# A fused GNN and mixture-of-experts kernel: six chunks of rows fetched one row at a time by the sync engine

## The reference

```python
def _L0_gnn_ref(node_repr, weight, bias, edge_index, edge_types):     # 53125 edges, 8 relations
    h_all = jnp.einsum('ni,roi->rno', node_repr, weight)
    src, dst = (edge_index[0], edge_index[1])
    msgs = h_all[edge_types, src]
    messages = jax.ops.segment_sum(msgs, dst, num_segments=node_repr.shape[0])
    return messages + bias
...
edge_index = jnp.stack([src, dst])
x = x + _L0_gnn_ref(_layernorm(x, axis=-1), L0_gnn_weight, L0_gnn_bias, edge_index, edge_type_8)
x = x + _L0_ffn_ref(_layernorm(x, axis=-1)[None], L0_ffn_gate_w, L0_ffn_gate_b, L0_ffn_w1, L0_ffn_w2, L0_ffn_w3)[0]
```

## Time and profile before

| | us |
|---|---|
| three runs | 925.81, 927.8, 933.22 |
| their median | 927.8 |
| the profiled execution's own time | 927.84 |
| its span in the profile | 926.1 |
| mean granted TensorE clock, as a share of full speed | 0.928 |

### The profile page before, as it was taken

One profiled execution on the slowest core, in us unless ns is written; L12 is line 12 of the kernel. 1 busy time (PEld: TensorE's weight loads), 2 busy tenths in 40 slices (PEclk: granted clock), 3 DMA queues, 4 the chain that ended last, 5 costly groups with the idle time before them and its releaser, 6 DMA issues.

```text
span 926.1 us, 17827 instructions
## 1 busy us (share of the span) xinstructions
PE 725.9 (78%) x4528; PEld 617.5 (67%) x4529; DVE 520.1 (56%) x1447; ACT 300.0 (32%) x466; POOL 659.9 (71%) x614
## 2 busy tenths in 40 slices
PE   0135778888887898877889887388999999999980
PEld 0123567666776677766777666267888888888870
DVE  6687746465454654546554577883444444344438
ACT  5423233252222433234332333222333333233323
POOL 7774777777777777777777760249788796987772
PEclk9997799899998999989999999589999999999995
DMA  9872444454444433343334334166756664763546
GB/s 207 245 224 63 146 145 145 144 178 145 144 144 137 133 104 103 106 130 107 102 106 131 106 95 147 34 203 236 222 186 227 205 197 167 229 210 95 158 135 188
DMA packets 91487, 141.91 MB, mean 153 GB/s; under 512 B 13197, under 2 KB 65889, under 8 KB 91456
## 3 DMA queue, kind: packets, MB, share of 16 engines
q0 software_dynamic: 25680, 70.16, 26.2%
q1 hardware_dynamic: 48854, 56.28, 18.9%
q10 hardware_dynamic: 16922, 15.15, 5.1%
HBM read 108.61 MB, written 32.93 MB: 153 GB/s over the span
## 4 chain that ended last, share of the span: by engine, by line
PE 39%; POOL 25%; issue 17%; DMA 11%; DVE 3%; ACT 2%; SPq 1%; DVEq 1%; POOLq 0%; ACTq 0%
POOL got L573 21%; PE ps L1677 15%; PE ps L1659 8%; PE ps L1525 8%; DMA got<-x_tab,gidx 5%; PE ps L1537 5%; DMA acc<-in_x 2%; PE ps L1685 2%; POOL x_sb L618 2%; DMA store<-in_L_gnn_weight 2%; PE ps L1643 1%; DVE ps L1450 1%; POOL part L607 1%; DMA y_tab<-ffn 1%; DMA x_tab<-x_sb 1%
## 5 line engine op out<-in xcount | busy, mean ns | idle before, releaser
L573 POOL DMA_INDIRECT got<-x_tab,gidx x388 | 370.9, 956 | 127.1 <-issue 113.1
L1525 PE MATMUL ps<-hot,got 125*128 125x256 f16 x1700 | 222.0, 292 | 88.3 <-DMA got<-x_tab,gidx 69.7
L1525 PEld LDWEIGHTS ps<-hot,got 125*128 125x128 f16 x1700 | 172.9, 104 | 133.2 <-issue 45.9
L1095 DVE TENSOR_TENSOR store<-store,ps 128x512 f32 x150 | 102.6, 684 | 187.8 <-PE ps L1525 153.2
L1677 PE MATMUL ps<-part,operands 128*128 x696 | 180.7, 409 | 5.3 <-POOL part L607 4.1
L1537 PE MATMUL ps<-part,store 128*128 128x256 f32 x800 | 183.7, 388 | 0.5 <-DVE acc L1106 0.5
L1537 PEld LDWEIGHTS ps<-part,store 128*128 128x128 f32 x800 | 154.0, 195 | 21.0 <-issue 0.5
L1677 PEld LDWEIGHTS ps<-part,operands 128*128 128x128 f32 x696 | 129.6, 193 | 33.4 <-issue 6.1
L1077 DVE TENSOR_SCALAR hot<-key_row,pass,drel 125x256 f16<-125x256 f16 x425 | 124.4, 358 | 11.2 <-issue 11.1
L1659 PE MATMUL ps<-part,operands 128*128 x696 | 97.8, 289 | 3.2 <-DVE operands L1389 3.2
L607 POOL TENSOR_TENSOR part<-store,part 128x2048 fp32r<-128x2048 f32 (+1 forms) x28 | 98.0, 3499 | 2.3
(11 more groups left out here) (250 smaller groups left out, 658.0 us busy)
## 6 DMA issues: line engine op xcount, KB each, us to landing
store<-in_L_ffn_w SPq DMA_DIRECT2D x48, 512.0 KB
y_tab<-ffn SPq DMA_DIRECT2D x9, 896.0 KB, 4.5
y_tab<-ffn ACTq DMA_DIRECT2D x58, 128.0 KB
xs_tab<-x_sb SPq DMA_DIRECT2D x14, 512.0 KB, 3.2
ffn<-xs_tab ACTq DMA_DIRECT2D x55, 128.0 KB
got<-x_tab,gidx POOLq DMA_INDIRECT x388, 2.7
acc<-in_x SPq DMA_DIRECT2D x5, 560.0 KB
x_tab<-got SPq DMA_DIRECT2D x5, 560.0 KB
```

Source lines behind the costliest of these rows:

```text
L573: nc.gpsimd.indirect_dma_start(got[:, c, :], None, x_tab, bass.IndirectOffsetOnAxis(ap=gidx[:, col:col + 1], axis=0)).then_inc(gathered[g] ...
L1095: v.tensor_tensor(window, window, ps[:, WIN_BANK[g], :].rearrange("p (q n) -> p q n", n=WIN), ALU.add).then_inc(win_added, 1)
L1525: last = mm(ps[:, WIN_BANK[g], k * KEYS:(k + 1) * KEYS], got[0:CE, c, a * DIM + k * P:a * DIM + (k + 1) * P], hot[0:CE, g % HOT, c - c0, : ...
```

## The change

Column 15 of the even turns 12, 14, 16, 18, 20 and 22 is no longer gathered by Pool. SyncE loads the 125 source numbers of such a chunk into registers, 25 at a time, and issues a DMA of one row (1 KB, one partition) for each. The rows go to `far_room`, two places of one chunk each that take turns, in memory that held the sort keys and the bias before. TensorE waits for all 125 rows (`far_in`) and takes the weights of that chunk from `far_room`. For that its loop over pairs is written twice: pairs 1 to 5 without, pairs 6 to 11 with the new operand, whose address comes from a register. SyncE may fill a place again once the last group of the turn that used it is done: chunks 2 to 5 wait for turns 12, 14, 16 and 18. The `y_tab` stores are let go two to a turn, and the first four batches of `store_x2` now stand behind the new loop.

```diff
@@ sync engine
-                sp.wait_ge(moved_on, n + 2)
+                sp.wait_ge(moved_on, n // 2 + 2)
...
+            sp.wait_ge(edges_done, 1)
+            far_chunks = early[FAR_FIRST:FAR_FIRST + 2 * FAR, HELD - 1, :].rearrange("(t a) e -> t a e", a=2)[:, 0, :]
+            sp.dma_start(far_src, far_chunks).then_inc(early_in, 16)
+            sp.wait_ge(early_in, 3 * 16)
             sp.wait_ge(counts_ready, 5)
...
+            for n in range(X_LOADS):
+                sp.wait_ge(batch_moved[n], 4 * 16)
+            rows_at = [sp.alloc_register(f"row_at{n}") for n in range(ROWS_AT)]
+
+            def far_rows(m, v0):
+                for p0 in range(0, CE, ROWS_AT):
+                    sp.reg_load(rows_at, far_src[m:m + 1, p0:p0 + ROWS_AT])
+                    for n, row in enumerate(rows_at):
+                        at = nc.s_assert_within(sp.snap(row, min_val=0, max_val=NODES - 1), 0, NODES - 1,
+                                                skip_runtime_bounds_check_because="sources are nodes")
+                        sp.dma_start(far_room[p0 + n:p0 + n + 1, m % 2, :], x_tab[bass.ds(at, 1), :]).then_inc(far_in, 16)
+
+            with sp.Fori(0, visits, TILES) as v0:
+                for m in range(FAR):
+                    freed = FAR_FIRST + 2 * (m - 2) + 1 if m >= 2 else 0
+                    sp.wait_ge(group_done, (v0 + freed) * NG + NG)
+                    sp.sem_inc(tiles_begun, 1)
+                    far_rows(m, v0)
+                    sp.wait_ge(far_in, (v0 // TILES * FAR + m + 1) * CE * 16)
+                    sp.sem_inc(tiles_begun, 1)
 
             for n in range(X_LOADS - 1):
                 store_x2(n)
@@ Pool
-                    for c in range(c0, min(c1, HELD - turn % 2)):
+                    for c in range(c0, min(c1, HELD - (turn % 2 or turn in range(FAR_FIRST, FAR_LAST + 1)))):
@@ TensorE, window
+                elif far:
+                    pe.wait_ge(far_in, (sweep * FAR + pair - FAR_FIRST // 2 + 1) * CE * 16)
+                    pe.wait_ge(held_ready, v0 + turn + 1)
+                    far_at = pe.snap(pair % 2, min_val=0, max_val=1)
...
+                            d0 = a * DIM + k * P
+                            rows = got[0:CE, c, d0:d0 + P]
+                            if far and c == HELD - 1:
+                                rows = far_room[0:CE, bass.ds(far_at, 1), d0:d0 + P].rearrange("p s d -> p (s d)")
@@ TensorE, the loop
-                    with nc.Fori(1, TILES // 2, engines=PE_ONLY, hint_back_edge=True, head_slot={pe.engine: 0}) as pair:
-                        for at in range(2):
-                            turn(pair * 2 + at, at, pair)
+                    for p0, p1, far in ((1, FAR_FIRST // 2, False), (FAR_FIRST // 2, TILES // 2, True)):
+                        with nc.Fori(p0, p1, engines=PE_ONLY, hint_back_edge=True, head_slot={pe.engine: 0}) as pair:
+                            for at in range(2):
+                                turn(pair * 2 + at, at, pair, far=far)
```

More of the change, by code:

```diff
@@ L61 @@
 EARLY = TILES + ODD
+FAR_FIRST, FAR = 12, 6
+ROWS_AT = 25
+FAR_LAST = FAR_FIRST + 2 * (FAR - 1)
 HOT = NG
@@ L184, in build @@
         key_c, bias = early_room[:, 0:CHUNKS], early_room[:, CHUNKS:CHUNKS + DIM]
+        far_room = early_room[:, 0:2 * DIM].bitcast(F16).rearrange("p (s d) -> p s d", s=2)
+        far_src = early_room[0:FAR, 2 * DIM:2 * DIM + CE].bitcast(I32)
         drel = sb("drel", [P, CHUNKS])
@@ L285, in build @@
         early_in = sem("early_in")
+        far_in = sem("far_in")
         early_rows = sem("early_rows")
@@ L1507, in _, with window @@
                 turn_weights(n)
-            def window(v0, turn, g, sweep=0, pair=0, odd=False):
+            def window(v0, turn, g, sweep=0, pair=0, odd=False, far=False, passed=0):
                 c0, c1 = GROUPS[g]
@@ L1518, in window @@
                     pe.wait_ge(held_ready, v0 + turn + 1)
+                elif far:
+                    pe.wait_ge(far_in, (sweep * FAR + pair - FAR_FIRST // 2 + 1) * CE * 16)
+                    pe.wait_ge(held_ready, v0 + turn + 1)
+                    far_at = pe.snap(pair % 2, min_val=0, max_val=1)
                 else:
-                    pe.wait_ge(gathered[g], (sweep * (TILES - ODD) + pair + 1) * 16)
+                    pe.wait_ge(gathered[g], (sweep * (TILES - ODD - FAR) + pair - passed + 1) * 16)
                     pe.wait_ge(held_ready, v0 + turn + 1)
@@ L1524, in window @@
                         for a in range(2):
-                            last = mm(ps[:, WIN_BANK[g], k * KEYS:(k + 1) * KEYS], got[0:CE, c, a * DIM + k * P:a * DIM + (k + 1) * P],
+                            d0 = a * DIM + k * P
+                            rows = got[0:CE, c, d0:d0 + P]
+                            if far and c == HELD - 1:
+                                rows = far_room[0:CE, bass.ds(far_at, 1), d0:d0 + P].rearrange("p s d -> p (s d)")
+                            last = mm(ps[:, WIN_BANK[g], k * KEYS:(k + 1) * KEYS], rows,
                                       hot[0:CE, g % HOT, c - c0, :], start=(c == c0 and a == 0), stop=(c == c1 - 1 and a == 1))
@@ L1582, in _, with turn @@
                         window(v0, 1, g)
-                    def turn(i, at, pair, norm=True):
+                    def turn(i, at, pair, norm=True, far=False):
                         window(v0, i, 3)
                         window(v0, i, 4)
-                        window(v0, i, 5, sweep, pair, odd=at == 1)
+                        window(v0, i, 5, sweep, pair, odd=at == 1, far=far and at == 0)
                         if norm:
@@ L1604, in _ @@
                     window(v0, t, 4)
-                    window(v0, t, 5, sweep, ODD)
+                    window(v0, t, 5, sweep, ODD, passed=FAR)
                     pe.wait_ge(choice_step, (b * GEN_W + w) * SWEEP_STEPS + 2 * CHOICE_STEPS)
```

## The result

The changed kernel takes 1057.1 us (median of 4 runs) against 927.5 (4 runs): a ratio of 1.1395, 95% interval 1.1357 to 1.1433. It is 130 us slower; the forecast was 1005 with an upper end of 1047. The direction was right and the time was 10 us outside the range. The profiled execution took 1056.1 us, its span is 1054.4.

A forecast was written before the change was run, and what follows sets the result against it. Pool bounded the edge stage; SyncE's row DMAs were to become the bound, moving the stage's end from 554.85 to 633 us. 927.84 + 78 = 1006, given as 1005; range 919 to 1047, the forecast's own 966 to 1047.

The forecast's parts named there:

- Pool sets the edge stage's pace, and six gathers less are worth up to 7.5 us.: Edge stage, second half: Pool waits for nobody, one gather per 1.25 us; removing six takes 7.5 us off the end.
- one queue of six that ends at the later of 191.5 + 6T and 321.1 + 4T: SyncE's six chunks, begun at 191.5 us, third not before turn 12 ends at 321.1; predicted end 601.3 us.
- T: SyncE's time for one chunk of 125 rows, loads and last landing included: 68.3 us, from 47.6 to 79.0.
- A row: 0.518 us.: SyncE's price per one-row DMA: issue 0.33, register calculation 0.054, MOVE 0.029, three gaps of 0.035; bounds 0.353 to 0.604.
- The lower bound of T: Cheapest chunk on SyncE: 125 x 0.353 + 3.5 = 47.6 us, with no register work at all.
- The loads: 5 x 0.307 = 1.5 us.: SyncE's five loads of 25 source numbers a chunk, priced like single-value loads; at 25 loads' price, 32 us more.
- a rival at 0.05: "Worse": a load costs as 25 loads, or SyncE waits for its instructions; T = 100, total 1195; chance 0.05.
- The upper end, 1047.: Top of the range for the total, at T = 75: stage ends at 673, +119.
- The stage's end, 32 us behind the late group.: Edge stage ends at 633, after turn 22's last group waits for SyncE's queue to end at 601.3: +78 us.
- The expert stage as before.: After the edge stage: the expert stage was expected to have its old length.
- y_tab's stores, `store_x2` and the doubled loop at nothing.: Two y_tab stores a turn, store_x2 behind SyncE's last chunk, TensorE's loop written twice: all covered by slack, taken as nothing.
- the rows just fit: SyncE issues a row in at most 0.344 us, T under 46.5, no chunk late, total 920; chance 0.19.

The follow-up runs named there:

- The run with aligned loads: Changed kernel with each set of 25 source numbers beginning at a multiple of 32 numbers instead of 25: 996.5 us against 931.5, ratio 1.0709.
- the other kernels with 382 gathers: Four variants of the changed kernel: loads realigned (996.5 us), one plain DMA a chunk (926.2), 105 DMAs a chunk (962.9), Pool's code padded with semaphore increments (1054.4).

## Why the prediction was right or wrong

- *Pool sets the edge stage's pace, and six gathers less are worth up to 7.5 us.* Right in kind: where the rows are in time the last gather starts 4.8 us earlier for six gathers fewer (or 7.0, less the 2.2 of the later start), 2.9 for two, 3.6 for four.
- *SyncE becomes the bound; one queue of six that ends at the later of 191.5 + 6T and 321.1 + 4T.* Right, in both regimes. With the measured T = 74.2 it gives 636.7; TensorE's last late group began at 638.7. At T = 55.5 the second term held to the tenth, with the release taken from that trace.
- *A row: 0.518 us.* Too dear. It measured 0.416. The instructions were the right ones (0.044 and 0.029 us), but a DMA of one row holds the sequencer 0.225 us, below the 0.300 that I took as the floor. I had excluded anything cheaper than the cheapest issue of the trace, all of which spread over 12 to 128 partitions, though I named the row as the smallest transfer there is. Size alone isn't the reason either: one DMA of 125 rows with fixed addresses took 0.250 us in the run with one DMA a chunk. Over a chunk: 125 x 0.102 = 12.8 us too many. The lower bound of T rested on the same floor; it was no bound.
- *The loads: 5 x 0.307 = 1.5 us.* This is the step that failed, the largest error in the sum. They take 3 x 5.34 + 1.80 + 1.90 = 19.7. I had bounded a load by one load of one value (0.27) and by 25 of them (6.8), a span of 32 us a chunk and of some 190 us on the total, and took the cheap end with the argument that it is one instruction, where a range should have held both. The dear end was priced alone, as a rival at 0.05, and left out of the range. 5.34 lies near it. The run with aligned loads, 1.9 us each, took 996.5 us, inside the forecast's range.
- Together T came out at 68.3 for 74.2, and 6 x 5.9 = 35 us on the queue. Two errors of 13 and 18 us a chunk nearly cancelled; that was luck, and the 1005 was closer than its terms.
- *The upper end, 1047.* It stood on T = 75, and T measured 74.2, so T alone didn't break the range: with it the prediction's own formula gives 191.5 + 445.2 + 32 = 668.7, and 1042. What came on top, and had no room in the range, are the next two terms and 2 us between the formula's 636.7 and 638.7.
- *The stage's end, 32 us behind the late group.* It was 36.4. TensorE comes out of 41 us of waiting at the low clock and stays there until 643.4 us, so Pool's first gather follows the late group's start by 5.7 us instead of 2.7; the last start of Pool was 23.7 us behind the first (I had 25); and TensorE ended 7.0 us after it instead of 3.9, with the "issue" wait of 1.7 us among them.
- *The expert stage as before.* 8.0 us longer here, 1.1 to 7.5 in the other kernels with 382 gathers. The prediction put it at nothing without a reason. The waits that hold it are named above, their first cause is open.
- *y_tab's stores, `store_x2` and the doubled loop at nothing.* The first and the third right, each by its own run. `store_x2` behind the last chunk: its eight issues took 7.1 us, not 2.8, and were over 29 us before the stage was; no run moved it alone.
- The rival "the rows just fit" needed 0.344 us a row and 3.5 us beside it. Against 0.416 and 22 us it was out by both terms. The sentence of the Trainium skill that issue time is usually small relative to the DMA ("DMA: Bandwidth & Descriptors", "Issuing engines are not separate DMA queues") would have given 920. The run with one DMA a chunk, 926 us, shows where it holds (0.25 us of issue, 3.1 of waiting for the landing); 125 rows a chunk show where not: there SyncE's instructions are nearly the whole price. The prediction said so of the trace of before, which has no DMA of one row; it was an argument then.

The sum of the misses: 37.4 on the queue (638.7 for 601.3), 4.7 behind it, 8.0 in the expert stage, together 50, which is 1056 - 1006.

## What to carry to other kernels

Price a job that moves to a sequencer by its whole instruction list, loads of registers too, and compare the time of one round with the distance in time between its deadlines: here 74 us against 38, and against the 46.5 that the early start allowed, so it had to fail, and fewer and wider spaced rounds (64 against 77) gave a small gain. Where a term has bounds that are a factor of twenty-five apart and it repeats 30 times on the path, the range must hold both, and no small list of existing rows gives a floor for a form that isn't in it.

## What the runs showed of the hardware

- A load of 25 numbers into registers takes 1.67 to 1.93 us when it begins at byte 0, 400 or a multiple of 128 of the table's row, and 5.34 at byte 100, 200 or 300. The fast starts are multiples of 16 bytes from the table's start, and the fast sets cross no multiple of 128 bytes; other steps weren't tried. An estimate from these rows: 5.34 / 25 = 0.21 us for each number, near the 0.26 of a load of one.
- The issue of a DMA with a register address on SyncE took 0.225 us for one row of 1 KB; with fixed addresses it took 0.267 for five rows in five partitions, 0.250 for 125 rows in 125 partitions, and 0.318 for a store from 112. The number of rows doesn't order these.
- SyncE issuing 750 one-row DMAs did not slow Pool's own: from 195 to 340 us, where Pool does not wait for rows of SyncE, the median from gather to gather is 1.25 us beside them and before.
